# Mamba's SiLU taken from ScalarE's table in four bursts a group, 14 instead of 15 of 32 state pairs read out by GpSimd, and the conditioning products in wide form

## The chip, the cores and the metric

The kernel runs on one core of a Trainium2 chip. The core has TensorE (PE, with its weight loads PEld), VectorE (DVE), ScalarE (ACT), GpSimd (POOL) and the DMA queues, issued here by SyncE (SP) and at the start by ScalarE. All of them run at the same time, each in the order of its own program, and wait for each other by semaphores. The metric is the device time of one execution in microseconds (us); everything is float32.

## The reference, cut to what matters

`x` is 64 sequences of 128 steps and 512 channels. Layer 0 is a Mamba block with adaptive layer norm, layer 1 an attention block with FiLM; the change touches layer 0 only.

```python
ada = silu(c) @ ada_w.T + ada_b                     # c: 64 x 1024, ada: 64 x 1536
shift, scale, gate = split(ada, 3)
xn = layernorm(x) * (1 + scale) + shift
x_in, z = split(xn @ in_proj_w.T, 2)                # 1024 inner channels each
u  = silu(causal_conv4(x_in) + conv_b)
dt_r, B, C = split(u @ x_proj_w.T, [64, 80])        # 16 states
dt = softplus(dt_r @ dt_proj_w.T + dt_proj_b)
for t in range(128):                                # for each channel and state
    h = h * exp(dt_t * A) + (dt_t * u_t) * B_t
    y_t = sum_n h * C_t
y  = (y + u * D_param) * silu(z)
x1 = x + gate * (y @ out_proj_w.T)
out = attention_with_film(x1, c, mask)              # layer 1, unchanged
```

## The kernel before

**Layer 0** works on 32 groups of two sequences (`GB = 2`, 256 columns). A group has 64 slots `q`: four quarters `j` of 256 channels each, and in each quarter 16 states. Two neighbouring states are a pair, so there are 32 pairs a group and eight in a quarter. For each slot ScalarE writes a decay, exp(dt * A), in two instructions into one of four PSUM banks (`decay`, L488, tile `dA`); VectorE runs the recurrence over it in one scan of 512 columns (L732). For each pair GpSimd forms dt * u * B for both states (`scale_b`, L782, tile `dbu`, a ring of four). The finished pair is multiplied by C either on VectorE (a "D" pair: the scan stays in `dA`, product at L660 into `hC`) or on GpSimd (a "G" pair: the scan goes to `hS`, product at L793). `KINDS` says which, for each quarter. TensorE then adds `hC` or `hS` up in PSUM by transposing products (L338, tile `Y`).

A decay bank is free again when its scan is done (G) or when the product of its pair is done (D): `bank_freed` is ScalarE's wait for that. GpSimd may form `dbu` of pair p when the scans of pair p - 4 are done, and needs `du` (= dt * u, L703) of the quarter.

**Side work** of the neighbouring groups fills the same slots. `SIDE` lists it, with the slots in which TensorE issues the parts: XN (transposed norm), XI (first half of in_proj), Z (its second half), CV (the convolution), XP (x_proj), DT (dt_proj), O (out_proj). All of it goes through three PSUM banks in turn (`side`); the next user of a bank waits until ScalarE or VectorE has emptied it. Where ScalarE and VectorE take up such a piece is set by offsets from its last slot (`A_AFTER`, `D_AFTER`, `DU_AFTER`, `DT_COPY`) and by the tables `YZ_AT`, `YT_AT`, `YF_AT`, `UD_AT`, `DMM_AT` and `Q_*`. Each engine's program goes through the slots in order, so a wait in one place holds up all that stands behind it on that engine.

SiLU is x / (1 + exp(-x)). For Z and CV ScalarE computes the second factor in three steps (`staged`): exp(-x) (L532, L535), ln(1 + t) (L545), exp(-t) (L551), and VectorE multiplies (L681 into `zs`, L686 into `u`). Softplus of DT is |x|, exp, ln on ScalarE (L539, L543, L549) and max + add on VectorE (L691). All these functions lie in one table of ScalarE, so it is loaded once.

**Before the groups**, `setup` makes scale and shift for all 64 sequences on TensorE (L1369), as 64 products with 128 columns of the weight held and 64 columns streamed; VectorE turns them into `gm0` and `bm0` (L1400 to L1405). The first bodies (`at` -2 and -1) prepare group 0. **Layer 1** starts when layer 0 has ended; its chain runs on TensorE.

Of the kernel before, what the change touches and what calls it, by code (L numbers as in the profile page):

```python
# [5 lines left out]
F32 = mybir.dt.float32  # L6
# [37 lines left out]
def slot_free(i, table):  # L44
# [8 lines left out]
KINDS = ["GGDGDGDD", "GGDGDGDD", "GGDGDGDD", "GDGDDGDD"]  # L53
# [6 lines left out]
D_ACC = {4: [9, 12, 17, 18], 5: [8, 10, 12, 16, 18]}  # L60
G_ACC = {4: [8, 11, 14, 18], 3: [9, 11, 17]}
# [68 lines left out]
def mamba(nc, ctx, NG, W, C, M, io, shared, edge, x_loaded, win_z_in, win_in):  # L130
# [16 lines left out]
    tmp = [sb(f"tmp{i}", [P, D]) for i in range(2)]  # L147
# [184 lines left out]
    def _(pe):  # L332
# [41 lines left out]
        def piece(kind, j, out, part, own, par):  # L374
# [9 lines left out]
            elif kind == "Z":  # L384
                if isinstance(own, int) and own == 0 and j == 0 and part == 0:
                    pe.wait_ge(win_z_in, 16 * KD)
                b, hf = Z_BLOCK[j]
                last = pe.matmul(out[:, :], xnF[par][:, part, b * P:(b + 1) * P],  # L388
                                 W["in"][:, part, DI + hf * D:DI + (hf + 1) * D], start=(part == 0), stop=(part == KD - 1))
            elif kind == "O":  # L390
                if part % 2 == 0:
                    wait(pe, yzf_done, own * 4 + (part // 2 + 1))
                last = pe.matmul(out[:, :], yzF[part // 2][par if part < 4 else 0][:, part % 2, j, :], W["out"][:, part, :], start=(part == 0), stop=(part == KI - 1))  # L393
# [83 lines left out]
        pe.wait_ge(init_done, 6)  # L477
# [3 lines left out]
    def _(act):  # L481
        act.preload_act_table_set("natural_log_exp_and_others")
        act.wait_ge(init_done, 6)
# [8 lines left out]
        def simple(kind, j, src, own, par, part, last):  # L492
# [1004 lines left out]
```

## Time and profile before

| | us |
|---|---|
| median of three runs | 4740.08 (4734.71 to 4741.60) |
| the profiled execution's own time | 4739.39 |
| its span, first to last instruction | 4737.5 |
| first scan of layer 0 | 88.9 |
| last readout of layer 0 on GpSimd begins | 3589.8 |
| first weight product of layer 1 | 3606.5 |

The span divides into a start of about 89 us, the 32 groups of layer 0 up to about 3592 us, and layer 1. The parts of the page say, for each engine, how much of the span it was busy; a table by stage says the same for one stretch, and there an engine that is busy for the whole stretch is the candidate for the bound. A list of waits says who waited for whom. Records of one engine can overlap by a little, since the next instruction starts before the one ahead has quite ended; so the cost of one more instruction is the distance between two starts and not the mean duration of a record.

### The profile page before, as it was taken

How to read it: one execution, taken by the hardware profiler on the slowest of the kernel's cores; microseconds unless marked ns; L12 is line 12 of the kernel's file. 1: busy time of each engine (PE TensorE's matmuls, PEld its weight loads, DVE VectorE, ACT ScalarE, POOL GpSimd, SP SyncE). 2: the span in 40 equal slices, each digit the busy share in tenths (PEclk: the TensorE clock that was granted, in tenths of full speed). 3: DMA queues.
4: the chain of work that ended last, by engine and by line, in shares of the span. 5: the costliest groups of instructions: out<-in, count | busy, mean ns of one | idle time of the engine just before them, and what ended most of it. 6: DMA issues, size and time to landing. Idle time of an engine off the chain costs nothing. (4 is left out here: it accounts for less than half of the span.)

```text
span 4737.5 us, 74634 instructions
## 1 busy us (share of the span) xinstructions
PE 4324.2 (91%) x21520; PEld 3105.0 (66%) x21520; DVE 4100.3 (87%) x5030; ACT 3283.7 (69%) x7747; POOL 3852.8 (81%) x1764
## 2 busy tenths in 40 slices
PE   8898899898898988999999989888978999999998
PEld 6666666666666666666666666666665666666665
DVE  2999999999999999999999999999987666666665
ACT  3888888888888888888888888878864334343343
POOL 1999999999999999999999999999995333333332
PEclk9999999999999999999999999999999999999999
DMA  4111111111111111111111111111123223232231
GB/s 167 41 46 48 46 46 48 45 54 59 56 53 46 46 48 46 46 48 46 48 58 58 59 46 46 45 48 46 43 76 135 88 89 105 88 99 89 89 105 47
DMA packets 123161, 301.00 MB, mean 64 GB/s; under 512 B 15489, under 2 KB 20865, under 8 KB 122818
## 3 DMA queue, kind: packets, MB, share of 16 engines
q1 hardware_dynamic: 120050, 296.73, 18.5%
q8 instruction: 157, 2.57, 0.2%
q14 instruction: 186, 1.52, 0.1%
q10 hardware_dynamic: 2768, 0.17, 0.0%
HBM read 245.35 MB, written 51.51 MB: 63 GB/s over the span
## 5 line engine op out<-in xcount | busy, mean ns | idle before, releaser
L782 POOL TENSOR_TENSOR dbu<-du,bc 128x1024 f32<-128x1024 f32 x1024 | 2477.9, 2537 | 101.1 <-DMA bc<-b_scratch 86.0
L488 ACT ACTIVATE dA<-dt,c_A 128x256 f32<-128x256 f32 x4096 | 1698.5, 463 | 506.3 <-DVE hC L660 502.7
L732 DVE TENSOR_TENSOR_SCAN dA<-dA,dbu 128x512 f32<-128x512 f32 x1088 | 1288.9, 1212 | 29.9 <-ACT dA L488 28.7
L732 DVE TENSOR_TENSOR_SCAN hS<-dA,dbu 128x512 f32<-128x512 f32 x960 | 1157.6, 1212 | 94.1 <-POOL dbu L782 59.7
L793 POOL TENSOR_TENSOR hS<-hS,bc 128x1024 f32<-128x1024 f32 x480 | 1218.5, 2539 | 5.5 <-DVE hS L732 5.5
L338 PE MATMUL Y<-c_ident,hC 128*128 128x128 f32 x4352 | 581.5, 277 | 151.0 <-DVE hC L660 150.9
L338 PEld LDWEIGHTS Y<-c_ident,hC 128*128 128x128 f32 x4352 | 498.9, 142 | 287.9 <-DVE hC L660 206.7
L660 DVE TENSOR_TENSOR hC<-dA,bc 128x1024 f32<-128x1024 f32 x544 | 653.2, 1201 | 0.0
L338 PE MATMUL Y<-c_ident,hS 128*128 128x128 f32 x3840 | 509.6, 277 | 1.1 <-POOL hS L793 1.1
L412 PE MATMUL side<-xin,c_conv_w 128*128 128x256 f32 x2048 | 499.7, 378 | 0.7 <-DVE zs L681 0.7
L388 PE MATMUL side<-sh_weights,sh_tile 128*128 128x512 f32 x1024 | 497.7, 604 | 0.0
L338 PEld LDWEIGHTS Y<-c_ident,hS 128*128 128x128 f32 x3840 | 454.2, 144 | 59.6 <-issue 41.7
L405 PE MATMUL side<-sh_tile,sh_weights 128*128 128x256 f32 x2048 | 470.8, 383 | 9.0 <-ACT sh_tile L499 7.3
L393 PE MATMUL side<-c_out_w,yzF 128*128 128x512 f32 x1024 | 477.4, 593 | 0.7 <-ACT yzF L572 0.7
L952 PE MATMUL pair<-sh_weights,p_xnF 128*128 128x512 f32 x1024 | 460.0, 592 | 0.0
L412 PEld LDWEIGHTS side<-xin,c_conv_w 128*128 128x128 f32 x2048 | 372.1, 189 | 98.8 <-issue 58.2
L405 PEld LDWEIGHTS side<-sh_tile,sh_weights 128*128 128x128 f32 x2048 | 382.4, 192 | 69.3 <-ACT sh_tile L499 12.8
L1283 POOL TENSOR_TENSOR p_q<-p_q,p_qmax 128x512 f32<-128x512 f32 x64 | 67.0, 1048 | 348.8 <-DVE p_qmax L1234 348.8
L1273 POOL TENSOR_TENSOR p_xr<-p_xr,p_bo_all 128x512 f32<-128x512 f32 x64 | 79.8, 1267 | 308.3 <-DMA p_xr<-x_scratch 308.3
L952 PEld LDWEIGHTS pair<-sh_weights,p_xnF 128*128 128x128 f32 x1024 | 189.7, 190 | 201.1 <-issue 199.4
L393 PEld LDWEIGHTS side<-c_out_w,yzF 128*128 128x128 f32 x1024 | 181.2, 190 | 140.1 <-issue 135.8
L388 PEld LDWEIGHTS side<-sh_weights,sh_tile 128*128 128x128 f32 x1024 | 182.7, 194 | 115.0 <-issue 109.8
(141 smaller groups left out, 5412.8 us busy)
## 6 DMA issues: line engine op xcount, KB each, us to landing
bc<-b_scratch SPq DMA_DIRECT2D x256, 512.0 KB, 3.7
sh_tile<-in_x SPq DMA_DIRECT2D x64, 512.0 KB, 6.1
o_scratch<-oS SPq DMA_DIRECT2D x64, 256.0 KB, 2.0
sh_tile<-o_scratch SPq DMA_DIRECT2D x32, 512.0 KB, 4.7
sh_tile<-gate_scratch SPq DMA_DIRECT2D x32, 512.0 KB, 5.6
p_xr<-x_scratch SPq DMA_DIRECT2D x32, 512.0 KB, 6.8
out<-p_xr SPq DMA_DIRECT2D x32, 512.0 KB, 2.9
x_scratch<-p_x_in SPq DMA_DIRECT2D x31, 512.0 KB, 3.1
```

What stands on the lines that cost most here:

```text
L338: last = pe.matmul(Y[:, b, k * P:(k + 1) * P], src[:, n, k, b * P:(b + 1) * P], C["ident"][:, :], start=False, stop=False, is_transpose=Tr ...
L388: last = pe.matmul(out[:, :], xnF[par][:, part, b * P:(b + 1) * P], W["in"][:, part, DI + hf * D:DI + (hf + 1) * D], start=(part == 0), st ...
L393: last = pe.matmul(out[:, :], yzF[part // 2][par if part < 4 else 0][:, part % 2, j, :], W["out"][:, part, :], start=(part == 0), stop=(pa ...
L405: last = pe.matmul(out[:, half * GT:(half + 1) * GT], W["in"][:, k, e * P:(e + 1) * P], xnF[par][:, k, :], start=(k == 0), stop=(k == KD - 1))
L412: last = pe.matmul(out[:, half * GT:(half + 1) * GT].rearrange("p (b t) -> p b t", b=GB), W["conv"][:, e, t, :], xin[j % 2][:, half, :, t: ...
L488: last = act.activation(dA[:, q % A_RING, e, :], dt[j % 2][:, e, :], ACT.Exp, scale=C["A"][:, 2 * j + e, n:n + 1])
L660: dve.tensor_tensor(hC[C_SLOT[i]][:, :, :, :], dA[:, k:k + 2, :, :], bc[:, 1, n:n + 2, :].unsqueeze(2).broadcast_to([P, 2, 2, GT]), ALU.mu ...
L732: dve.tensor_tensor_scan(out.rearrange("p e t -> p (e t)"), dA[:, q % A_RING, :, :].rearrange("p e t -> p (e t)"), dbu[(q // 2) % B_RING][ ...
L782: gps.tensor_tensor(dbu[p % B_RING][:, :, :, :], du[j % 2][:, :, :].unsqueeze(1).broadcast_to([P, 2, 2, GT]), bc[:, 0, n:n + 2, :].unsquee ...
L793: gps.tensor_tensor(h, h, bc[:, 1, n:n + 2, :].unsqueeze(2).broadcast_to([P, 2, 2, GT]), ALU.mult).then_inc(hcP_done, 1)
L952: last = pe.matmul(out[:, :], lhs(k), w[:, k, :], start=(k == 0), stop=(k == KD - 1))
L1273: gps.tensor_tensor(xr[:, b, :], xr[:, b, :], bo[:, :], ALU.add).then_inc(s["xb_done"], 1)
```

## The change

- `KINDS` has 14 G pairs and 18 D pairs a group (15 and 17 before), in another pattern; the fourth `hS` buffer goes with it.
- SiLU of Z and CV is one function of ScalarE, straight from PSUM into `zs` and `u`. It lies in another table than exp and ln, so `BURSTS` puts one Z and one CV together at four slots of a group, with a table load ahead of them and one behind. VectorE has no part in it any more. Z is cut by quarters instead of by sequence and half.
- An `hC` product follows the second scan of its pair directly (`R_AFTER = 1`; it stood one scan later). The DT step and `du` stand in the same slot.
- All tables of slots are new. `tmp` is one tile, `yzF` is single except for quarter 0.
- In `setup` the conditioning products hold the 64 sequences and stream 512 columns of the weight (16 products); VectorE copies the result to SBUF and TensorE turns it back (eight transposes). The clearing of rows of the dt weight moves from the start of `mamba` to `setup`.

```diff
-KINDS = ["GGDGDGDD", "GGDGDGDD", "GGDGDGDD", "GDGDDGDD"]
+KINDS = ["GGDGGDDD", "GDGDGDDD", "GDGDGGDD", "GDGDDDGD"]
-D_ACC = {4: [9, 12, 17, 18], 5: [8, 10, 12, 16, 18]}
+D_ACC = {4: [9, 14, 19, 19], 5: [10, 10, 13, 13, 18]}
...
+    ("Z", 1, 0, [0, 0, 1, 2]),
+    ("CV", 1, 1, [0, 0, 1, 2]),
...
+    ("O", 0, -1, [9, 9, 9, 9, 10, 10, 10, 10]),
...
+    ("DT", 0, 1, [49]),
+    ("CV", 0, 2, [53, 53, 54, 54]),
+    ("Z", 0, 1, [53, 54, 55, 55]),
...
+BURSTS = [
+    (6, [("Z", 1, 0), ("CV", 1, 1)]),
+    (22, [("Z", 2, 0), ("CV", 2, 1)]),
+    (36, [("CV", 3, 1), ("Z", 3, 0)]),
+    (58, [("Z", 0, 1), ("CV", 0, 2)]),
+]
...
+STEP1, STEP2, DT_AFTER, DU_AFTER, COPY_AFTER = 1, 2, 4, 4, 7
+R_AFTER = 1
+YZ_AT = [20, 33, 52, 68]
-S_RING = 3
+S_RING = 4
...
+        def take_functions(name):
+            if functions[0] != name:
+                act.preload_act_table_set(name)
+                functions[0] = name
...
+        def soft(kind, j, src, own, par):
+            if kind == "Z":
+                take_functions(SILU)
                 wait(act, filled[kind], nth(kind, j, own))
+                wait(act, yz_done, own * 4 + j - 1)
+                act.activation(zs[j % 2][:, :, :].rearrange("p b c -> p (b c)"), src[:, :], ACT.Silu).then_inc(zs_done, 1)
+            elif kind == "CV":
+                take_functions(SILU)
+                wait(act, filled[kind], nth(kind, j, own))
...
+                for e in range(2):
+                    last = act.activation(u[par][:, 2 * j + e, :], src[:, e * GT:(e + 1) * GT], ACT.Silu,
+                                          bias=C["cb"][:, 2 * j + e:2 * j + e + 1])
...
-                        t = 16 * j + 2 * p + 2
+                        t = 16 * j + 2 * p + R_AFTER
                         if q == t % UNITS and inside(at, -(t // UNITS)):
                             readout(g - t // UNITS, j, m)
...
-                    last = pe.matmul(ps[:, i, k, :], ada[:, c, s:s + P], cT[:, c, :],
-                                     start=(c == 0 and i == 0 and k == 0), stop=(c == KC - 1), skip_group_check=True)
+                last = pe.matmul(ps[i][0:NB, :], cT[:, c, :], ada[:, c, i * D:(i + 1) * D], start=(c == 0), stop=(c == KC - 1))
...
+        dve.memset(W["dt"][RANK:XD, :], 0.0)
+        for i in range(2):
+            dve.wait_ge(mod_done, i + 1)
+            dve.tensor_copy(mod[0:NB, i, :], ps[i][0:NB, :]).then_inc(mod_copied, 1)
+        dve.wait_ge(mod_turned, 2)
```

What the order on ScalarE was at slots 16 to 26 of group 0 (dA is the decays, four instructions for two slots; L535, L545 and L551 are the three steps of a CV piece, L539, L543 and L549 those of a DT piece, L572 copies `Y` out):

```order
L488 ACTIVATE dA<-dt1,c_A 128x256 x4
L565 ACTIVATE uD<-u0,c_dcol 128x256 x2
L488 ACTIVATE dA<-dt1,c_A 128x256 x4
L535 ACTIVATE tmp1<-side0,c_ncb 128x256 x2
L488 ACTIVATE dA<-dt1,c_A 128x256 x4
L545 ACTIVATE tmp1<-tmp1 128x512
L551 ACTIVATE tmp1<-tmp1 128x512
L488 ACTIVATE dA<-dt1,c_A 128x256 x4
L572 ACTIVATE yzF00<-Y 128x512
```

And now, at slots 16 to 25 (L547 and L554 are the SiLU of Z and CV, L591 the copy of `Y`, L628 and L630 belong to the norm):

```order
L504 ACTIVATE dA<-dt1,c_A 128x256 x16
L495 ACT_TABLE_LOAD
L547 ACTIVATE zs0<-side2 128x512
L554 ACTIVATE u1<-side1,c_cb 128x256 x2
L591 ACTIVATE yzF0a<-Y 128x512
L495 ACT_TABLE_LOAD
L628 ACTIVATE lnv<-mv,c_eps 128x2
L630 ACTIVATE rstd<-lnv 128x2
L504 ACTIVATE dA<-dt1,c_A 128x256 x4
```

The steps of CV stood one by one between the decays; now a block with two table loads stands between the decays of slot 23 and those of slot 24.

VectorE at slots 22 to 26 of group 0, before (the rows named after three tensors, into `dA` or `hS`, are scans; `hC1` and `hC2` are products of D pairs):

```order
L732 SCALAR_TENSOR_TENSOR hS0<-dA,dbu3 128x512
L660 TENSOR_TENSOR hC1<-dA,bc 128x1024
L732 SCALAR_TENSOR_TENSOR hS0<-dA,dbu3 128x512
L732 SCALAR_TENSOR_TENSOR dA<-dA,dbu0 128x512 x2
L732 SCALAR_TENSOR_TENSOR hS1<-dA,dbu1 128x512
L660 TENSOR_TENSOR hC2<-dA,bc 128x1024
```

And now, at slots 22 to 25:

```order
L729 SCALAR_TENSOR_TENSOR dA<-dA,dbu3 128x512
L748 BN_AGGR mv<-stats 128x2 x2
L729 SCALAR_TENSOR_TENSOR dA<-dA,dbu3 128x512
L678 TENSOR_TENSOR hC2<-dA,bc 128x1024
L729 SCALAR_TENSOR_TENSOR hS2<-dA,dbu0 128x512 x2
```

Before, the product of a D pair stood behind the first scan of the pair after it (`hC1` behind a scan into `hS0`); now it stands right behind the second scan of its own pair.

ScalarE at the start of group 0, before (L557 is the copy of dt, L499 the norm of the next group):

```order
L549 ACTIVATE tmp0<-tmp0 128x512
L557 ACTIVATE dt0<-side2 128x4x127
L488 ACTIVATE dA<-dt0,c_A 128x256 x4
L499 ACTIVATE sh_tile2<-side0,c_bm0,c_gm0 128x128 x2
L499 ACTIVATE sh_tile2<-side1,c_bm0,c_gm0 128x128 x2
```

And now:

```order
L570 ACTIVATE tmp<-tmp 128x512
L576 ACTIVATE dt0<-side2 128x4x127
L495 ACT_TABLE_LOAD
L547 ACTIVATE zs0<-side0 128x512
L515 ACTIVATE sh_tile2<-side1,c_bm0,c_gm0 128x128 x2
L515 ACTIVATE sh_tile2<-side2,c_bm0,c_gm0 128x128 x2
L495 ACT_TABLE_LOAD
L504 ACTIVATE dA<-dt0,c_A 128x256 x4
```

Two table loads, a SiLU of Z and half of the norm now stand ahead of the first decays of the layer.

## Rows read from the trace of the kernel before

**Rows 1.** Table by stage: each engine's busy time in each stretch, then clock, DMA.

```profile
core 0: us, PE busy (x) PEld busy (x) DVE busy (x) ACT busy (x) POOL busy (x), PEclk, DMA share, GB/s
...
1000.00:1500.00 500.00, 454.42 (x2394) 338.04 (x2393) 486.02 (x503) 412.03 (x955) 500.00 (x217) 0.99 0.14 46
```

**Rows 2.** Timeline of POOL: start, duration, line, operation, tiles, count.

```profile
1000.14 6.97 POOL L782 TENSOR_TENSOR dbu<-du,bc 128x1024 f32<-128x1024 f32 x3
1007.08 2.35 POOL L793 TENSOR_TENSOR hS<-hS,bc 128x1024 f32<-128x1024 f32 x1
```

**Rows 3.** Table by stage, one period of a group.

```profile
1002.39:1111.22 108.83, 98.68 (x522) 73.70 (x521) 105.91 (x110) 89.03 (x207) 108.83 (x48) 0.98 0.15 50
```

**Rows 4.** Who waited for whom, VectorE, 300 to 3300 us: total us, times, longest.

```profile
DVE hS L732 <- POOL dbu L782: 55.8, 54, 1.5
DVE hS L732 <- ACT dA L488: 14.6, 15, 1.2
DVE dA L732 <- ACT dA L488: 9.6, 27, 0.4
```

**Rows 5.** Groups by line, that same period: count | busy us, mean ns | idle before.

```profile
L488 ACT ACTIVATE dA<-dt,c_A 128x256 f32<-128x256 f32 x128 | 53.1, 463 | 15.0 <-DVE hC L660 15.0
L551 ACT ACTIVATE tmp<-tmp 128x512 f32<-128x512 f32 x8 | 5.0, 625 | 0.1
L545 ACT ACTIVATE tmp<-tmp 128x512 f32<-128x512 f32 x8 | 5.0, 620 | 0.0
```

**Rows 6.** Timeline of ACT in layer 1, around a table load.

```profile
3700.49 0.63 ACT L1078 ACTIVATE p_hF<-p_hp 128x512 f32<-128x512 f32 x1 [0.57 <-DVE p_hp L1154]
3701.14 1.28 ACT L1079 ACT_TABLE_LOAD   x1
3702.43 1.08 ACT L1083 ACTIVATE p_qF<-pair 128x512 f32<-128x512 f32 x2
```

**Rows 7.** Timeline of DVE in that period.

```profile
1048.86 0.85 DVE L686 SCALAR_TENSOR_TENSOR u<-side,c_cb,tmp 128x256 f32<-128x256 f32 x2
1049.63 2.33 DVE L732 TENSOR_TENSOR_SCAN dA<-dA,dbu 128x512 f32<-128x512 f32 x2
1051.88 0.67 DVE L681 TENSOR_TENSOR zs<-side,tmp 128x512 f32<-128x512 f32 x1
1052.47 1.21 DVE L732 TENSOR_TENSOR_SCAN dA<-dA,dbu 128x512 f32<-128x512 f32 x1
1053.59 1.20 DVE L660 TENSOR_TENSOR hC<-dA,bc 128x1024 f32<-128x1024 f32 x1
```

**Rows 8.** Timeline of DVE: the last pair of layer 0.

```profile
3592.17 1.22 DVE L732 TENSOR_TENSOR_SCAN dA<-dA,dbu 128x512 f32<-128x512 f32 x1
3593.42 1.22 DVE L660 TENSOR_TENSOR hC<-dA,bc 128x1024 f32<-128x1024 f32 x1
```

**Rows 9.** Timeline of the start, all engines.

```profile
6.62 27.54 PE L1369 MATMUL mod<-c_cT,ada 128*128 128x64 f32 x128 [6.62 <-DMA ada<-in_adaT]
...
34.28 1.10 DVE L1400 TENSOR_SCALAR t<-mod,c_one_plus,c_cols 128x64 f32<-128x64 f32 x4 [6.93 <-PE mod L1369]
...
38.75 0.91 DVE L649 MEMSET c_dt_w<- 32x1024 f32 x1 [0.27 <-issue]
...
39.72 1.97 PE L399 MATMUL side<-c_ident,sh_tile 128*128 128x128 f32 x8 [5.55 <-DVE c_dt_w L649]
```

**Rows 10.** Timeline, waits of DVE and POOL in group 0 and in the last group.

```profile
108.31 2.35 DVE L732 TENSOR_TENSOR_SCAN dA<-dA,dbu 128x512 f32<-128x512 f32 x2 [11.13 <-ACT dA L488]
...
110.74 2.35 POOL L782 TENSOR_TENSOR dbu<-du,bc 128x1024 f32<-128x1024 f32 x1 [5.81 <-DVE dA L732]
...
3536.53 2.35 POOL L782 TENSOR_TENSOR dbu<-du,bc 128x1024 f32<-128x1024 f32 x1 [8.44 <-DVE du L703]
```

**Rows 11.** Chain that ended last, in order of time: start, us, what.

```profile
3674.05 13.73 PE pair L952 x32
```

More of the change, by code:

```diff
@@ L120 @@
 C_RING = 3
-S_RING = 3
+S_RING = 4
 C_SLOT = [i % C_RING for i in range(ND)]
-S_SLOT = [(G_BASE[j] + i + sum(j >= at for at in (1, 3)[:-NGP % S_RING])) % S_RING for j in range(4) for i in range(len(G_PAIRS[j]))]
+S_SLOT = [(G_BASE[j] + i + j * (-NGP % S_RING) // 3) % S_RING for j in range(4) for i in range(len(G_PAIRS[j]))]
 PAIRS = UNITS // 2
+LOG_EXP, SILU = "natural_log_exp_and_others", "silu_and_others"
 FAR = 1e30
@@ L146, in mamba @@
     u = [sb(f"u{i}", [P, KI, GT]) for i in range(2)]
-    tmp = [sb(f"tmp{i}", [P, D]) for i in range(2)]
     xd = sb("xd", [XD + 1, GT])
@@ L386, in piece @@
                     pe.wait_ge(win_z_in, 16 * KD)
-                b, hf = Z_BLOCK[j]
-                last = pe.matmul(out[:, :], xnF[par][:, part, b * P:(b + 1) * P],
-                                 W["in"][:, part, DI + hf * D:DI + (hf + 1) * D], start=(part == 0), stop=(part == KD - 1))
+                for k in two:
+                    last = pe.matmul(out[:, half * 2 * P:(half + 1) * 2 * P], xnF[par][:, k, half * P:(half + 1) * P],
+                                     W["in"][:, k, DI + j * 2 * P:DI + (j + 1) * 2 * P], start=(k == 0), stop=(k == KD - 1))
             elif kind == "O":
@@ new lines, in softplus @@
+        def softplus(step, j, src, own):
+            take_functions(LOG_EXP)
+            if step == 0:
+                wait(act, filled["DT"], nth("DT", j, own))
+                wait(act, dt_done, own * 4 + j)
+                act.activation(tmp[:, :], src[:, :], ACT.Abs).then_inc(abs_done, 1)
+            elif step == 1:
+                wait(act, abs_done, own * 4 + (j + 1))
+                act.activation(tmp[:, :], tmp[:, :], ACT.Exp, scale=-1.0).then_inc(exp_done, 1)
+            else:
+                wait(act, exp_done, own * 4 + (j + 1))
+                act.activation(tmp[:, :], tmp[:, :], ACT.Ln, bias=1.0).then_inc(log_done, 1)
@@ L639, in body @@
                 beside(q + 1)
+            if inside(at, 0):
+                take_functions(LOG_EXP)
         over_groups(act, body)
@@ L697, in make_gate, with step @@
             dve.tensor_tensor(oS[1][0:NB, :], dA[0:NB, 3, :, :].rearrange("p e t -> p (e t)"), oS[0][0:NB, :], ALU.add).then_inc(gate_v, 1)
+        def step(j, src, own):
+            wait(dve, log_done, own * 4 + (j + 1))
+            dve.scalar_tensor_tensor(src[:, :], src[:, :], 0.0, tmp[:, :], ALU.max, ALU.add).then_inc(dt_done, 1)
         def step_times_u(j, src, own, par):
@@ L752, in body @@
                     last.then_inc(stats_done, 1)
-                for (kind, j, d, end, bk, s, off), of, go in side:
-                    if kind == "DT" and q == end + DU_AFTER - off:
+                for (kind, j, d, end, bk, off), of, go in side:
+                    if q == end + DT_AFTER - off:
+                        step(j, bank[bk], go + d)
+                    if q == end + DU_AFTER - off:
                         step_times_u(j, bank[bk], go + d, (of + d) % 2)
-                    if kind in D_AFTER and q == end + D_AFTER[kind] - off:
-                        side_dve(kind, j, bank[bk], tmp[(sig_base[of] + s) % 2], go + d, (of + d) % 2)
         over_groups(dve, body)
```

203 lines of the change are left out of this document (76 added, 127 removed).

## The prediction

> **What bounds the kernel now.** I read the table by stage first. In the middle of layer 0 POOL is busy for 500.00 of 500 us, DVE for 486.02, PE for 454.42, ACT for 412.03 [rows 1]. The timeline of POOL shows no gap between its instructions: three take 6.94 us from start to start, 2.31 us each, whether it is a `dbu` or a readout [rows 2]. A group has 32 + 15 = 47 of them, and the period of a group is 108.83 us [rows 3], which is 47 x 2.315. So POOL sets layer 0. The second engine is close: DVE is busy for 105.91 us of that period [rows 3], and its waits over 300 to 3300 us are 55.8 us for POOL and 24.2 us for ACT's decays, in 27.6 periods 2.0 and 0.9 us each [rows 4]. ACT is busy for 89.03 us and waits 15.0 us for DVE to give back a decay bank [rows 3, 5]: it runs as far ahead as the four banks let it. Layer 1's chain is PE alone, 0.43 us a record of 512 columns, and is not touched [rows 11].
>
> **POOL.** One readout less a group: 46 x 2.315 = 106.5 us instead of 108.8. Over 32 groups that is **74.1 us**, as long as POOL never waits. Nothing in the change touches what one POOL instruction costs.
>
> **DVE.** Removed: four Z products at 0.59 us and four CV pairs at 0.77 us from start to start [rows 7], 5.4 us. Added: one more `hC` product, 1.12 us [rows 7]. There is an addition that the diff shows only as `R_AFTER = 1`: each `hC` now follows directly on the scan whose result it reads, and has to wait for its end. Where nothing depends, an instruction starts 1.12 us after the one ahead; the only place in before where a product follows its own scan is the last pair, and there it is 1.25 us [rows 7, 8]. Lower bound: 0, if the ring of scans hides it; upper 0.13. I take the one row: 18 x 0.13 = 2.3 us. The four `du` directly behind their DT step get the same, 0.5 us. Sum: 105.9 - 5.4 + 1.1 + 2.3 + 0.5 = **104.4 us** of 106.5. DVE is as nearly full as before, with 2.1 us a group to spare (2.9 before).
>
> **ACT.** Removed: L545 and L551 for Z and CV, 5.0 + 5.0 us a group [rows 5]. The first step becomes the SiLU, at the same size: in layer 1 a SiLU of 512 columns takes 0.63 us [rows 6]. Added: eight table loads a group. A load takes 1.28 us, begins 0.02 us after the SiLU ahead has ended, and the next instruction starts 0.01 us after it [rows 6]; eight are 10.4 us. Sum: 89.0 - 10.0 + 0.3 + 10.4 = 89.7 us, as much as before. What is new is that it comes in blocks of 1.28 + 0.6 + 0.8 + 1.28 = 4.0 us, in which no decay is made. The Trainium skill (ScalarE: Activation LUTs, What ACT_TABLE_LOAD costs) gives 1283 ns for the load, as here, and another 1380 ns of drain for every switch. By that, eight switches would be 21.3 us, ACT would have 100.7 us a group and a block would last 6.8 us; the row shows no such drain.
>
> **Does a block starve DVE?** I walk through the one at slot 22, which also has the copy of `Y` and the two norm steps. Let time 0 be the end of the `hC` product that frees the banks for slots 22 and 23. ACT: decays to 1.8 (53.1 / 128 = 0.415 us each [rows 5]), load to 3.0, Z to 3.6, CV to 4.4, copy to 5.0, load to 6.3, two small norm steps to 6.9, first decay of slot 24 ready at 7.7. DVE in that time: scan 20, the gate product, two norm statistics of 0.6, scans 21, 22, 23 and the next `hC`, 4 x 1.13 + 0.6 + 1.2 + 0.2 + 1.25 = 7.8. So it arrives just as the decay does; slot 26, whose banks come free only at 7.8 and behind which two more side steps stand, may cost 0.4. For slot 6 (block behind a G pair, which gives its banks back early) I get 6.3 for ACT and 6.4 for DVE, for slot 36 5.7 and 6.4, for slot 58 7.2 and 7.0. About 0.6 us of waits in sum, beside the 0.9 us that DVE waits for decays today [rows 4]. 104.4 + 1.0 to 1.5 = 105.4 to 105.9, under 106.5: POOL keeps the bound, with its `dbu` ring of four pairs between it and DVE's small delays. I allow 0.1 us a group for places where it doesn't, 3 us in all.
>
> **PE** has the same streaming as before (Z as 16 products of 256 instead of 4 of 512 columns in each quarter, at the same us per column), 98.7 us busy of then 106.5 [rows 3]. It has to finish Z and CV before their block; what a late one costs is a rival below.
>
> **Start.** The 64-column products of `setup` take 27.54 us, 0.43 us for each of 64 pairs of records [rows 9]. The wide ones are 16 pairs at 2 x 0.43 [rows 11], 13.8 us, and end near 20.4. DVE is ready at 34.28 - 6.93 = 27.35 [rows 9]; then come the clearing that moved here (0.91 [rows 9]), two copies near 0.7 each and four plus four transposes, about 1 us: 30.7 instead of 34.28, 3.6 us earlier. The 0.91 us clearing stood just ahead of the first transpose at 39.72 [rows 9] and is gone from there. Together -4.5. Up to the first `dbu` a CV loses two ScalarE steps and DVE's product (0.62 + 0.63 + 0.85, [rows 5, 7]), which counts for the last one; against that XI, its copy and CV of one quarter now follow each other on PE, four copies near 0.6 exposed. I take 0.
>
> **Group 0 pays.** Before, DVE waited 11.13 us and POOL 5.81 us here, as ACT stood at XI copies ahead of slot 4 [rows 10]. Now two loads, Z (which PE makes only behind the gate product) and half of the norm stand ahead of the first decay, and a head block and the block of slot 6 follow at once. Decays of slots 0 and 1 come about 11 us later after the end of the DT product than they did, the XI copies about 5 us later; three blocks then add some 8 us on ACT, of which its spare time gives back part. I take POOL's start as +9 us, with 3 to 15 as bounds. **Last group:** POOL waited 8.44 us for `du` [rows 10], as O and the FiLM product shared PE's slots 14 to 21 ahead of the DT product. O is now at 9 and 10; I take half of the wait, -4, bounds -8 to +4.
>
> **Sum.** Against the profiled execution: 4739.4 - 74.1 + 3 - 4.5 + 9 - 4 = 4668.8; the median of the runs is 0.7 above it, so **4670 us**.
>
> **The rivals.** (1) *DVE takes the bound.* It has 2.1 us a group to spare. If the waits for decays are 3.5 us a group (0.9 us a block), the period is 107.9 and the gain 30 us: 4712. For it: at slots 22 and 58 the two sides of the walk meet within 0.2 us, and 2.3 us of DVE's sum rest on one row. Against: the slots of the blocks stand where DVE has other work. Chance 0.18 for anything from 4690 to 4730. (2) *The blocks cost more than the gain*: slower than before. It decides from 108.8 - 104.4 = 4.4 us of waits a group, 1.1 us a block. It happens if PE delivers Z or CV late, since then ACT stands inside the block with SiLU's table loaded and no decay can be made: PE is 93% busy, and the block of slot 36 takes a Z whose last part PE issues at slot 36, just behind O 1 and CV 3. At 2 us late in each block: 104.4 + 1 + 8 = 113.4, +147 us, 4885 us. Chance 0.07. (3) *A table switch costs a drain in the middle of a busy ACT queue*, which the rows of layer 1, where ACT has idle time ahead, might not show: blocks of 6.8 us, 2.8 us late each, 104.4 + 1 + 11 = 116.4, +243 us, near 4980. This is the case that the page named above would give. Chance 0.03. (4) *The gain is given back in no measurable way* (group 0 worse than 15 us and DVE's waits near break-even together), 4731 to 4749: 0.04.
>
> **How the numbers follow.** POOL-bound: 0.68, from 4655 (group 0 +3, last group -8, no slack used) to 4685. With rival 1 the range to hold eight in ten is 4655 to 4722. A measurement of this kernel tells about 0.2% (9.5 us) from no change. Faster by more: 0.68 + 0.18 = 0.86; within: 0.04; slower: 0.10.
>
> **What the profile after would show.** Right: POOL busy all of a middle stretch with 46 instructions in 106.5 us; DVE near 104.4 busy; its waits for decays under 2 us a group; table loads of 1.28 us with no gap around them; first `dbu` near 82, and waits of POOL in group 0 of 20 us instead of 11. Wrong: any wait of POOL for DVE in the middle of layer 0 (rival 1); waits of ACT for PE inside a block (rival 2); a gap next to a load (rival 3); `hC` starting 1.12 us after its own scan would show DVE's sum 2.3 us too high.

## The result, and the profile after

The changed kernel takes **4697.39 us** (median of four runs, 4694.11 to 4699.91) beside 4737.96 us of the kernel before (median of four runs too, 4734.71 to 4741.60): ratio 0.9916, 95% interval 0.9904 to 0.9927. It is 0.84% or 40.6 us faster; 4670 was predicted, in a range of 4655 to 4722. The profiled execution took 4697.85 us, with a span of 4696.0.

A group in the middle, the row that answers to [rows 3] (us of PE, PEld, DVE, ACT, POOL, then clock and DMA):

```profile
2078.04:2184.60 106.56, 98.39 (x552) 80.42 (x552) 103.10 (x99) 90.89 (x199) 106.56 (x47) 0.98 0.15 51
```

The period is 106.56 us as forecast, and POOL has no gap in it. The page's rows of the `hC` products and of the table loads:

```profile
L678 DVE TENSOR_TENSOR hC<-dA,bc 128x1024 f32<-128x1024 f32 x576 | 705.2, 1224 | 64.9 <-DVE dA L729 15.5
...
L495 ACT ACT_TABLE_LOAD x263 | 337.4, 1283 | 12.3 <-PEq L1443 7.7
```

But not all groups are like that one. POOL's list of waits from 300 to 3300 us, which has no entry in the kernel before:

```profile
POOL dbu L779 <- DVE du L704: 25.0, 12, 2.9
POOL hS L790 <- DVE hS L729: 1.5, 4, 0.5
```

26.5 us, where the prediction allowed 3. In POOL's timeline they stand in pairs; one of the six pairs, behind an ordinary group:

```profile
2280.78 9.29 POOL L779 TENSOR_TENSOR dbu<-du,bc 128x1024 f32<-128x1024 f32 x4
...
2389.36 9.33 POOL L779 TENSOR_TENSOR dbu<-du,bc 128x1024 f32<-128x1024 f32 x4 [1.64 <-DVE du L704]
...
2417.35 9.31 POOL L779 TENSOR_TENSOR dbu<-du,bc 128x1024 f32<-128x1024 f32 x4 [2.44 <-DVE du L704]
```

The first of a pair is the first `dbu` of quarter 1, the second that of quarter 2, and pairs begin at 665, 1096, 1528, 1959, 2389 and 2819 us: every 431 us, which is four groups, and six times. The middle of the program is a loop over four groups with seven turns (`with eng.Fori(0, (NG - 4) // 4)`, bodies `at` 1 to 4), so it jumps back six times. What the engines do at that place, from 2357 us on (timelines of ACT, PE and DVE, one after the other):

```profile
2357.24 3.27 ACT L504 ACTIVATE dA<-dt,c_A 128x256 f32<-128x256 f32 x8
2363.40 1.67 ACT L504 ACTIVATE dA<-dt,c_A 128x256 f32<-128x256 f32 x4 [2.89 <-DVE dA L729]
...
2372.20 1.28 ACT L495 ACT_TABLE_LOAD   x1
2374.17 0.60 ACT L547 ACTIVATE zs<-side 128x512 f32<-128x512 f32 x1 [0.68 <-DVE yz L687]
...
2377.94 0.60 ACT L591 ACTIVATE yzF<-Y 128x512 f32<-128x512 f32 x1 [2.13 <-PE Y L378]
...
2364.43 3.43 PE L395 MATMUL side<-sh_weights,sh_tile 128*128 128x256 f32 x8 [5.08 <-issue]
...
2366.71 4.57 DVE L729 TENSOR_TENSOR_SCAN hS<-dA,dbu 128x512 f32<-128x512 f32 x4 [2.48 <-ACT dA L504]
```

"issue" is idle time in which nothing that the profile shows was waited for. TensorE stands 5.08 us, and its next eight products take 3.43 us instead of 1.89, as the granted clock is 0.58 behind the stop, between its levels of 1.2 and 2.4 GHz (0.5 and 1.0); from 2368 us on it is 1.00. The table by stage has it in the third column from the end:

```profile
2364.00:2368.00 4.00, 3.57 (x10) 2.96 (x11) 1.52 (x3) 3.49 (x10) 4.00 (x3) 0.58 0.51 180
```

ScalarE issues no decay for 2.9 us. The profile puts this down to a scan (`<-DVE dA L729`), which had ended at 2362.88; in a group without a jump there is no stop at this place, and twelve decay instructions follow each other (experiment 1). DVE gets its decays 2.48 us late, then waits 0.99 us for TensorE ahead of the gate product and 2.01 us behind the block of slot 6. That block lasts from 2372.20 to 2379.85, 7.65 us instead of 4.4, as the `Y` copy in it waits 2.13 us for TensorE. So DVE comes 5.0 us late to `du`, here that of quarter 2, in the group ahead and in this one (period 106.56 us):

```profile
2305.01 0.69 DVE L704 TENSOR_TENSOR du<-side,u 128x512 f32<-128x512 f32 x1
...
2416.58 0.69 DVE L704 TENSOR_TENSOR du<-side,u 128x512 f32<-128x512 f32 x1
```

The parts, against the kernel before:

| | forecast | measured | from |
|---|---|---|---|
| one readout less, 32 groups | -74.1 | -73.8 | POOL's 32 groups without their waits, 3411.2 instead of 3485.0 us |
| start, up to the first `dbu` | -4.5 | -3.5 | 82.99 instead of 86.47 us |
| POOL's waits in group 0 | +9 | +7.2 | 19.4 instead of 12.2 us |
| POOL's waits in the middle | +3 | +26.5 | the list above |
| POOL's waits in the last groups | -4 | +1.0 | 9.5 instead of 8.4 us |
| behind POOL's last instruction of layer 0 | 0 | +1.1 | 1146.5 instead of 1145.4 us |
| sum | -70.6 | -41.5 | 41.5 between the profiled executions |

### The profile page after: what moved, and what is told of

It reads as the page before. It is cut to its first block and busy times, and to the rows that moved or that the text cites. A ratio compares the mean times of both kernels' runs of the same rounds, so it can differ in the third digit from the quotient of the medians.

```text
span 4696.0 us, 75508 instructions
## 1 busy us (share of the span) xinstructions
PE 4326.6 (92%) x22456; PEld 3319.5 (71%) x22456; DVE 4017.1 (86%) x4680; ACT 3351.9 (71%) x7497; POOL 3779.0 (80%) x1732
## 5 line engine op out<-in xcount | busy, mean ns | idle before, releaser
L779 POOL TENSOR_TENSOR dbu<-du,bc 128x1024 f32<-128x1024 f32 x1024 | 2391.2, 2359 | 118.1 <-DMA bc<-b_scratch 82.5
L729 DVE TENSOR_TENSOR_SCAN dA<-dA,dbu 128x512 f32<-128x512 f32 x1152 | 1355.1, 1212 | 26.2 <-POOL dbu L779 21.1
L729 DVE TENSOR_TENSOR_SCAN hS<-dA,dbu 128x512 f32<-128x512 f32 x896 | 1040.6, 1205 | 63.5 <-ACT dA L504 49.2
L790 POOL TENSOR_TENSOR hS<-hS,bc 128x1024 f32<-128x1024 f32 x448 | 1057.0, 2359 | 19.9 <-DVE hS L729 19.9
L678 DVE TENSOR_TENSOR hC<-dA,bc 128x1024 f32<-128x1024 f32 x576 | 705.2, 1224 | 64.9 <-DVE dA L729 15.5
L345 PEld LDWEIGHTS Y<-c_ident,hC 128*128 128x128 f32 x4608 | 534.7, 145 | 111.9 <-DVE hC L678 94.7
L345 PEld LDWEIGHTS Y<-c_ident,hS 128*128 128x128 f32 x3584 | 416.7, 144 | 181.8 <-POOL hS L790 157.5
L395 PE MATMUL side<-sh_weights,sh_tile 128*128 128x256 f32 x2048 | 504.7, 388 | 27.8 <-issue 27.8
L395 PEld LDWEIGHTS side<-sh_weights,sh_tile 128*128 128x128 f32 x2048 | 386.1, 195 | 79.2 <-issue 30.0
L412 PEld LDWEIGHTS side<-sh_tile,sh_weights 128*128 128x128 f32 x2048 | 385.1, 195 | 61.8 <-issue 10.3
L400 PE MATMUL side<-c_out_w,yzF 128*128 128x512 f32 x896 | 399.3, 596 | 0.7 <-ACT yzF L591 0.7
L495 ACT ACT_TABLE_LOAD x263 | 337.4, 1283 | 12.3 <-PEq L1443 7.7
```

Source lines behind the costliest of these rows:

```text
L345: last = pe.matmul(Y[:, b, k * P:(k + 1) * P], src[:, n, k, b * P:(b + 1) * P], C["ident"][:, :], start=False, stop=False, is_transpose=Tr ...
L395: last = pe.matmul(out[:, half * 2 * P:(half + 1) * 2 * P], xnF[par][:, k, half * P:(half + 1) * P], W["in"][:, k, DI + j * 2 * P:DI + (j ...
L400: last = pe.matmul(out[:, :], yzF[part // 2][par if part < 2 else 0][:, part % 2, j, :], W["out"][:, part, :], start=(part == 0), stop=(pa ...
L412: last = pe.matmul(out[:, half * GT:(half + 1) * GT], W["in"][:, k, e * P:(e + 1) * P], xnF[par][:, k, :], start=(k == 0), stop=(k == KD - 1))
L495: act.preload_act_table_set(name)
L678: dve.tensor_tensor(hC[C_SLOT[i]][:, :, :, :], dA[:, k:k + 2, :, :], bc[:, 1, n:n + 2, :].unsqueeze(2).broadcast_to([P, 2, 2, GT]), ALU.mu ...
```

## The experiments

Medians are of the runs of a kernel; ratios are to runs of the kernel before on the same chip, with 95% intervals. "Without the loop" means that the 28 middle groups are written out.

**1. No loop, and twice the jumps.** The edit, for all engines at once:

```
-        with eng.Fori(0, (NG - 4) // 4) as i:
-            for at in range(1, 5):
-                body(i * 4 + at, at)
+        for at in range(1, NG - 3):
+            body(at, at)
```

> The changed kernel with the 28 middle groups written out instead of a loop of seven turns of four groups; every engine's instructions and tables are the same. Theory A (the loop's jump): in the trace of the changed kernel POOL waits for du twice after each of the six jumps back, 4.4 us a jump, because ACT issues nothing for about 2.9 us at the jump and the slack between du and its first use in the quarters 1 and 2 is smaller than that. Without jumps these waits go: 4697 - 26 = 4671 us, POOL without a wait from 130 to 3400 us. Rival B (the waits come from something else that recurs every four groups, such as data or side work): 4697, the same waits at the same places. Rival C (the code written out has to be fetched all the time and costs more than the jumps): over 4697.

4670.12 us, ratio 0.9862 (0.9845 to 0.9878). POOL's list of waits from 300 to 3300 us is empty. At the same place of the program as above:

```profile
2338.39 4.87 ACT L503 ACTIVATE dA<-dt,c_A 128x256 f32<-128x256 f32 x12
2343.19 0.90 ACT L583 ACTIVATE uD<-u,c_dcol 128x256 f32<-128x256 f32 x2
...
2340.55 1.89 PE L394 MATMUL side<-sh_weights,sh_tile 128*128 128x256 f32 x8
```

ScalarE goes through from one group to the next with twelve decay instructions in a row where it had stopped after eight, and TensorE's products of `Z` 1 have no wait ahead of them. Theory A holds to 1 us, and B and C fall.

With a loop over two groups (`(NG - 4) // 2`, `range(1, 3)`), 13 jumps:

> The changed kernel with a loop of 14 turns of two groups instead of seven of four: 13 jumps back instead of 6. Theory A: seven more jumps at 4.4 us, 4697 + 31 = 4728 us, a pair of POOL waits for du every 217 us. Theory A with saved-up slack (DVE may need more than two groups to catch up): more than that, up to 4740. Rival B: 4697.

4726.98 us, ratio 0.9979 (0.9970 to 0.9989): 29.6 us for seven more jumps, 4.2 each, beside 27.3 us for the first six, 4.5 each. POOL's waits from 300 to 3300 us:

```profile
POOL dbu L779 <- DVE du L704: 42.4, 21, 2.8
POOL hS L790 <- DVE hS L729: 12.8, 13, 1.5
```

TensorE's idle time put down to issue is 27.8 us in 6 places in the changed kernel and 56.3 us in 13 here: 4.6 and 4.3 us a jump.

**2. The same in the kernel before.** The loop over two groups there:

> The kernel before with a loop of 14 turns of two groups instead of seven of four. Its POOL waits 0.9 us in sum in the middle of layer 0, though it makes the same jumps. Theory A: its slack (du of quarter 1 in slot 7 instead of 12) covers the jump, so seven more of them cost 0 to 2 us: 4738 to 4740. If the jump had a price by itself on POOL, 7 x 2 to 4 us: 4752 to 4768.

4733.65 us, ratio 0.9995 (0.9985 to 1.0004): nothing. This is ScalarE in the kernel before, at the jump:

```profile
2386.43 0.84 ACT L535 ACTIVATE tmp<-side,c_ncb 128x256 f32<-128x256 f32 x2 [0.18 <-PE side L412]
2389.79 1.67 ACT L488 ACTIVATE dA<-dt,c_A 128x256 f32<-128x256 f32 x4 [2.52 <-issue]
```

So a stop of 2.5 us was in the trace from which the prediction was made, and cost nothing there. The same place one group earlier, and TensorE at the jump, show why:

```profile
2279.68 1.67 ACT L488 ACTIVATE dA<-dt,c_A 128x256 f32<-128x256 f32 x4 [1.32 <-DVE hC L660]
...
2388.60 1.34 PE L338 MATMUL Y<-c_ident,hC 128*128 128x128 f32 x8 [2.21 <-DVE hC L660]
```

ScalarE stands there for a decay bank for 1.32 us in every group without a jump, and 1.9 to 2.5 us at the six jumps: a jump adds 0.6 to 1.2 us, DVE then waits as long for decays, and POOL not at all. TensorE stands 2.2 us for `hC` there in every group, with a jump or without; the stop of 4.2 to 5.1 us that it makes in the changed kernel is not in this trace. The new order has no idle time at that place on either engine, so the stops come through. Why TensorE's own stop is so much longer there is not shown.

**3. `du` earlier by moving the DT products.**

```
     ("Z", 1, 0, [0, 0, 1, 2]),
     ("CV", 1, 1, [0, 0, 1, 2]),
-    ("XI", 2, 1, [3, 5, 6, 8]),
-    ("DT", 1, 0, [8]),
+    ("DT", 1, 0, [3]),
+    ("XI", 2, 1, [7, 8, 8, 8]),
...
+    ("DT", 2, 0, [17]),
     ("Z", 2, 0, [18, 19, 19, 20]),
-    ("XI", 3, 1, [21, 21, 22, 22]),
-    ("DT", 2, 0, [24]),
+    ("XI", 3, 1, [23, 23, 24, 24]),
```

> The changed kernel with the DT product of quarter 1 at slot 3 instead of 8 and of quarter 2 at slot 17 instead of 24 (du then in slots 7 and 21 instead of 12 and 28), XI 2 and XI 3 behind them; the loop as it is. Theory A: POOL's waits for du in the middle (26.5 us), most of the 6.0 us of them in group 0 and of the 4.6 us in the last group go: 4697 - 26 - 4 - 3 = 4664 us. Rival D (DVE itself is the bound around a jump, and the waits for du only show it; DVE has 2 us a group to spare and the loss would come out elsewhere, as waits for scans): 4685 to 4697.

4844.60 us, ratio 1.0225 (1.0208 to 1.0242): far off both. The waits for `du` are gone from POOL's list, but TensorE's list from 300 to 3300 us now begins:

```profile
PE side L412 <- ACT zs L547: 130.5, 27, 4.9
```

The three side banks go round in the order of the list. By the swap `XI` 2 gets the bank of `Z` 1, which ScalarE empties only inside the block of slot 6. TensorE comes there before the block and stands 4.8 us in each group, with everything behind it. The edit did not only move `du`, so its time decides nothing about theory A; it shows what a late TensorE or a late block costs: 4.6 us a group. One thing can be read from it: with `du` of quarter 1 in slot 7, as in the kernel before, a group with a jump is still 5 us longer than its neighbours (116.5 us beside 111.5).

**4. Is the gain the readout alone?** The version without the loop, with quarter 1 of `KINDS` as before (15 G pairs):

```
-KINDS = ["GGDGGDDD", "GDGDGDDD", "GDGDGGDD", "GDGDDDGD"]
+KINDS = ["GGDGGDDD", "GGDGDGDD", "GDGDGGDD", "GDGDDDGD"]
```

> The changed kernel without the loop (4670 us), with 15 of 32 pairs on GpSimd as before the change (one D pair of quarter 1 becomes a G pair); SiLU, bursts, slots and setup stay new. Theory A (the gain of the middle is the one readout less, and nothing else): POOL is full again with 47 instructions of 2.315 us, 32 x 2.315 = 74 us more, 4744 us. Rival E (the new SiLU or the slots gain something by themselves): under 4735.

4740.21 us, ratio 1.0006 (0.9997 to 1.0016): 70.1 us more than with 14, of 74.1. New SiLU, blocks and slots bring nothing as long as POOL bounds; DVE's waits for decays, 2.3 us a group there from 1000 to 3000 us, cost nothing either. (Outside the middle, POOL's waits in the groups 0 and 31 also differ: 27.0 us here and 28 to 29 with 14.)

**5. Was the SiLU needed for it?** The kernel before with 14 G pairs, first with its loop, then without:

```
-KINDS = ["GGDGDGDD", "GGDGDGDD", "GGDGDGDD", "GDGDDGDD"]
+KINDS = ["GGDGDGDD", "GDGDGDDD", "GGDGDGDD", "GDGDDGDD"]
```

> The kernel before with 14 instead of 15 of 32 pairs on GpSimd, and nothing else changed: SiLU in three steps with VectorE's products. Theory A: POOL would need 106.5 us a group, but DVE needs 105.9 + 1.1 = 107.0 us and has 0.9 us of waits for decays: period 107.9 instead of 108.8, 4738 - 29 = 4709 us, DVE full and POOL waiting. If the slack of POOL's ring is not enough for two engines that are both full, 4715 to 4730. Rival F (POOL sets the time even so, and the SiLU part of the change was not needed): 4738 - 74 = 4664 us.

4767.86 us, ratio 1.0064 (1.0047 to 1.0081): slower than before, beyond what theory A allowed.

> The kernel before with 14 G pairs (4768 us with the loop) and the middle groups written out. In the trace of the version with the loop the period is 109.1 us in most groups and 1.5 to 2 us longer around a jump. Theory A (DVE is full there, so each of six jumps costs 2 to 4 us): 4743 to 4756 us, still not faster than before, with a period of 109.1 us: 107.0 of work and 2.2 us of waits for decays. If the 30 us by which it was slower than before came from the jumps alone: 4738 or less.

4728.26 us, ratio 0.9982 (0.9972 to 0.9991). One group of it:

```profile
2107.91:2216.85 108.94, 98.56 (x521) 73.64 (x521) 106.40 (x111) 88.81 (x207) 106.78 (x47) 0.98 0.15 49
```

DVE is full: 106.4 us busy, and 1.8 us of waits for decays a group (34.0 us in the 18.4 periods from 1000 to 3000 us), twice those of [rows 4]; that this is so because a D pair gives its banks back later than a G pair was not tested by itself. The row is of the longer kind of group: periods of 109.0 and 107.9 us (2.3 and 1.3 us of waits for decays) alternate, 108.5 in the mean instead of 108.9. The jumps cost 39.6 us here, 6.6 each, more than the forecast 2 to 4; they are spread over all four groups of a turn. So with this pattern and the old slots the readout gains 8 us (4728.3 beside 4736.5 on the same chip) without the loop and loses with it. DVE's part of the SiLU has to go before POOL's 106.5 us can be reached; what the whole change adds without the loop is 4728.3 - 4670.1 = 58 us. Other slots for the old SiLU were not tried.

**6. Is there room in the blocks?** Without the loop, and between the two SiLUs of a block:

```
+                            if i == 1:
+                                take_functions(LOG_EXP)
+                                act.activation(spare[:, :], C["eps"][:, :], ACT.Exp)
                             soft(kind, j, bank[bk], g + d, (at + d) % 2)
```

> The changed kernel without the loop (4670 us), in which each burst of two SiLUs is cut in two: behind the first SiLU the table of exp and ln is loaded, one exp of a single column runs into a spare tile, and SiLU's table is loaded again. That adds 2 x 1.28 us and about 0.2 us to each of the four blocks, as much as a drain at each of the eight switches would have. Theory A (the walk of the prediction: the sides meet within 0.2 to 1 us in the blocks): DVE waits about 2 us more in each block, 104.4 + 1 + 8 = 113 us a group, near 4880 us, 4840 to 4910. Rival G (the four banks and ACT's spare 17 us a group absorb it): DVE's 2.3 us a group of slack are not used up, 4670 to 4690.

4938.16 us, ratio 1.0424 (1.0407 to 1.0442), worse than theory A's range. A group takes 115.22 us:

```profile
2102.34:2217.56 115.22, 102.68 (x552) 85.22 (x552) 103.31 (x100) 101.92 (x211) 106.85 (x47) 0.94 0.14 47
```

and DVE's waits for decays from 1000 to 3000 us are

```profile
DVE hS L732 <- ACT dA L504: 148.0, 52, 3.0
DVE dA L732 <- ACT dA L504: 30.0, 33, 2.5
```

178 us in 17.4 periods, 10.3 us a group or 2.6 a block for 2.9 us of added length (7.35 instead of 4.43 us, each with one copy in it). The blocks have next to no room, as the walk said. ScalarE as a whole is not full (101.9 of 115.2 us), and that does not help.

**7. One more readout to VectorE.** Without the loop, 13 G pairs:

```
-KINDS = ["GGDGGDDD", "GDGDGDDD", "GDGDGGDD", "GDGDDDGD"]
+KINDS = ["GGDGDDDD", "GDGDGDDD", "GDGDGGDD", "GDGDDDGD"]
```

> The changed kernel without the loop (4670 us), with 13 instead of 14 pairs on GpSimd (one G pair of quarter 0 becomes a D pair). POOL needs 45 x 2.315 = 104.2 us a group. In the middle of the kernel without the loop DVE waits 2.3 us a group for POOL and 0.2 us for decays, so its own work is about 104.0 to 104.2 us; one more product makes 105.4. Theory A: DVE is the bound, 105.4 + 0.2 to 1 us of waits = 105.6 to 106.4 us a group, 4642 to 4667 us, and POOL waits 1 to 2 us a group. Rival (with both engines full the ring of four no longer covers, and decays come late since the bank of a D pair is free later): slower than 4670, up to 4700.

4662.90 us, ratio 0.9844 (0.9828 to 0.9861), a period of 105.93 us. The same with each `hC` product one scan later:

```
-R_AFTER = 1
+R_AFTER = 2
```

> The version without the loop and with 13 G pairs (4663 us, period 105.9 us, DVE full), with each hC product one scan later, as before the change (R_AFTER = 2). Theory H (the direct successor costs DVE 0.13 us for each of 19 products, and nothing else changes): DVE needs 2.4 us a group less, POOL's 104.2 us bound it, 4663 - 31 x 1.7 = 4610 us, at most 4625. Theory A (the four blocks on ACT have no room: a D pair that gives its two banks back 1.1 us later makes each block end 1.1 us later for DVE): 2.4 us gained and 4 x 1.1 us or more of new waits for decays, 4663 + 31 x 2 = 4725 us, from 4690 to 4760.

4847.61 us, ratio 1.0235 (1.0218 to 1.0252): the sign of theory A, with three times its price. DVE waits 151 us for decays from 1000 to 3000 us (1.2 before the edit). The two banks of a D pair come back later, and the blocks turn this into waits. Theory H's saving is there all the same: without its waits DVE needs 102.7 us a group instead of 105.2. Without `hC` directly behind its scan this version with the blocks is slower than the kernel before; the prediction had this placing only as a cost.

In the version with 13 G pairs POOL waits 1.6 us a group for a `du`. I took it for that of quarter 1 and moved its DT product:

```
-    ("XI", 2, 1, [3, 5, 6, 8]),
-    ("DT", 1, 0, [8]),
+    ("XI", 2, 1, [3, 5, 6, 7]),
+    ("DT", 1, 0, [7]),
```

> The version without the loop and with 13 G pairs (4663 us), with the DT product of quarter 1 at slot 7 instead of 8 (XI 2 ends at 7 too), so du of quarter 1 stands in slot 11 instead of 12. There POOL waits 1.6 us for du in each group, and DVE 0.7 us for POOL 19 slots earlier. Theory A: both go, the period is DVE's work alone, 105.9 - 0.7 = 105.2 us, 4663 - 22 = 4641 us. Rival I (DT 1 takes the side bank that the block of slot 6 frees; TensorE stands there until the block's end, so du comes no earlier, and the products behind come later): 4660 to 4690, with a wait of TensorE of 1 to 2 us a group at the DT product.

4665.38 us, ratio 0.9852 (0.9836 to 0.9869): no gain. The wait was for `du` of quarter 2, in slot 28 behind the block of slot 22, and the moved steps of ScalarE cost DVE 1.1 us of waits for decays. (`DT` 2 ends at slot 24, and DVE takes it up four slots later.) For quarter 2 VectorE alone is moved:

```
-                    if q == end + DT_AFTER - off:
+                    if q == end + DT_AFTER - (j == 2) - off:
                         step(j, bank[bk], go + d)
-                    if q == end + DU_AFTER - off:
+                    if q == end + DU_AFTER - (j == 2) - off:
```

> The version without the loop and with 13 G pairs (4663 us), in which VectorE takes the DT step and du of quarter 2 one slot earlier (27 instead of 28); ScalarE and TensorE as they are. In its trace POOL's wait of 1.6 us in each group is for this du, and ScalarE's last step for it ends 2.2 us before VectorE takes it up. Theory A: POOL's wait becomes 0.5 us, DVE's 0.7 us for POOL goes, period 105.9 - 0.7 = 105.2 us, 4663 - 22 = 4641 us. Rival J (the time comes back as DVE waits for decays behind the blocks, as when the DT product of quarter 1 was moved): 4655 to 4665 us.

**4625.77 us**, ratio 0.9768 (0.9752 to 0.9784), the fastest of all. A group before and after this edit, in the two versions:

```profile
2050.71:2156.64 105.93, 96.98 (x552) 79.02 (x552) 104.24 (x100) 90.52 (x199) 104.33 (x46) 1.00 0.15 51
```

```profile
2035.21:2140.32 105.11, 98.28 (x552) 80.57 (x552) 104.16 (x101) 90.55 (x199) 104.33 (x46) 0.98 0.15 51
```

DVE waits neither for POOL nor, but for 0.3 us in 2000, for ScalarE: its own work is the period. POOL's wait is 0.8 us a group. 0.82 us a group is 25 of the 37 us. Another 8.6 us are in the last group, where POOL's waits fall from 20.9 to 12.3 us; this was not expected.

## Why the prediction was right, and where it was off

**What bounds, and the readout: right.** POOL sets the period, 46 x 2.315 us, in every group without a jump, and experiment 4 gives 70 us for the one readout. As a whole the change is 0.84% faster where 1.4% were forecast: the mechanism held, and a term that the sum had nearly at nothing took 26.5 us back.

**VectorE's sum: right.** In the middle groups it waits 2.3 us a group for POOL and 0.2 for ACT in the version without the loop, so its own time is 106.6 - 2.5 = 104.1 us; 104.4 was forecast. It is busy for 103.1 us. The rest, 1.0 us, are short gaps ahead of the `hC` products. Where a scan, its neighbour and `hC` follow each other, `hC` starts 1.25 us after the second scan, as in [rows 8]:

```profile
2329.86 2.33 DVE L729 TENSOR_TENSOR_SCAN dA<-dA,dbu 128x512 f32<-128x512 f32 x2
2332.23 1.23 DVE L678 TENSOR_TENSOR hC<-dA,bc 128x1024 f32<-128x1024 f32 x1
2333.37 2.33 DVE L729 TENSOR_TENSOR_SCAN dA<-dA,dbu 128x512 f32<-128x512 f32 x2
```

2332.23 - 2329.86 is 2.37 for a scan at 1.12 and this step. That the step costs this much is shown by experiment 7, where DVE's own time falls by 2.5 us for 19 products when they stand one scan later. What the term left out is the other side of `R_AFTER = 1`: experiment 7 prices it at 185 us in the version with 13 G pairs.

**ScalarE and the blocks: right.** 90.9 us a group instead of 89.7, and a block without a wait, here with an `XI` copy in it:

```profile
2333.96 1.28 ACT L494 ACT_TABLE_LOAD   x1
2335.26 0.60 ACT L546 ACTIVATE zs<-side 128x512 f32<-128x512 f32 x1
2335.75 0.83 ACT L553 ACTIVATE u<-side,c_cb 128x256 f32<-128x256 f32 x2
2336.46 0.61 ACT L520 ACTIVATE xin<-side 128x512 f32<-128x512 f32 x1
2337.09 1.28 ACT L494 ACT_TABLE_LOAD   x1
```

A load starts 0.02 us after what is ahead of it and is followed at once, in a busy queue as in layer 1 [rows 6]. By these rows a switch costs 1.28 us. The Trainium skill (ScalarE: Activation LUTs, What ACT_TABLE_LOAD costs) adds 1380 ns of drain to each; no run here shows it. The rival built on it (4980 us) is answered by experiment 6, in which that much time was really added: 4938 us.

**The start: right within 1 us.** The wide products and what follows them:

```profile
6.58 16.70 PE L1365 MATMUL mod<-ada,c_cT 128*64 128x512 f32 x32 [6.58 <-DMA ada<-in_adaT]
...
28.21 0.91 DVE L1399 MEMSET c_dt_w<- 32x1024 f32 x1 [0.25 <-issue]
29.14 1.28 DVE L1402 COPY mod<-mod 64x512 f32<-64x512 f32 x2
...
31.20 1.10 DVE L1405 TENSOR_SCALAR t<-turned,c_one_plus,c_cols 128x64 f32<-128x64 f32 x4 [0.78 <-PE turned L1371]
...
35.46 1.97 PE L406 MATMUL side<-c_ident,sh_tile 128*128 128x128 f32 x8 [4.30 <-DVE xd L667]
```

The products end at 23.3 instead of 20.4 us (0.52 us a record where [rows 11] have 0.43), which is hidden. The chain goes on at 31.20 instead of 30.7, the first transpose starts 4.3 us earlier than in [rows 9], and 0.8 us of it are lost again before the first `dbu`.

**Group 0: right.** The timeline, with ScalarE's part first:

```profile
82.46 1.28 ACT L495 ACT_TABLE_LOAD   x1
89.07 0.60 ACT L547 ACTIVATE zs<-side 128x512 f32<-128x512 f32 x1 [5.33 <-PE side L395]
...
93.27 1.23 DVE L729 TENSOR_TENSOR_SCAN hS<-dA,dbu 128x512 f32<-128x512 f32 x1 [11.45 <-ACT dA L504]
...
107.21 2.34 DVE L729 TENSOR_TENSOR_SCAN hS<-dA,dbu 128x512 f32<-128x512 f32 x2 [11.02 <-ACT dA L504]
...
109.62 2.35 POOL L790 TENSOR_TENSOR hS<-hS,bc 128x1024 f32<-128x1024 f32 x1 [8.71 <-DVE hS L729]
```

SiLU's table is loaded and `Z` is not there: rival 2's mechanism, at the place where the prediction had put its price. POOL waits 19.4 us, 20 were forecast.

**The last group: wrong sign.** -4 was taken because `O` no longer shares TensorE's slots with the FiLM product. It is now `Z` 2, in slots 18 to 20, that shares them:

```profile
3478.08 0.60 ACT L547 ACTIVATE zs<-side 128x512 f32<-128x512 f32 x1 [5.27 <-PE side L395]
...
3484.08 2.34 DVE L729 TENSOR_TENSOR_SCAN hS<-dA,dbu 128x512 f32<-128x512 f32 x2 [6.86 <-ACT dA L504]
...
3486.50 2.37 POOL L790 TENSOR_TENSOR hS<-hS,bc 128x1024 f32<-128x1024 f32 x1 [2.10 <-DVE hS L729]
...
3492.51 9.28 POOL L779 TENSOR_TENSOR dbu<-du,bc 128x1024 f32<-128x1024 f32 x4 [3.64 <-DVE du L704]
```

The block waits 5.27 us with the wrong table loaded, and the waits for `du` come back behind it. The step did not ask which other pieces stand in the FiLM product's slots.

**The middle: the term that was mis-sized**, 3 us instead of 26.5. The sum was made from one period of 106.5 us and multiplied, and nothing in it was about the loop, though the stop of 2.5 us stands in the trace of before. That the loop is the cause is shown by experiment 1. The reason given for the 3 us was that the `dbu` ring of four pairs lies between POOL and DVE's small delays. It does for scans, but POOL cannot form a `dbu` without `du`, and `du` of quarter 2 is done only 0.5 us ahead of its first use in an ordinary group (2305.70 and 2306.25 us). It stood nearly as close in the kernel before (slot 28 in both, 0.7 to 1.0 us ahead). What is new is that DVE comes late: 5.0 us at the `du` of quarters 1 and 2 behind the jump at 2359 us (4.2 to 6.1 at the six jumps), from the three waits named in the section on the result, where in the kernel before no `du` of quarter 2 was late by as much as 0.2 us. POOL lost 4.4 us there: 0.35 us for a scan, 1.64 at quarter 1, whose `du` has 3.1 us to spare (2277.71 and 2280.78 us), and 2.44 more at quarter 2. The slot of `du` in quarter 1 did go from 7 to 12, but this only sets at which of the two quarters POOL stands first: a `du` of quarter 2 that is 5.0 us late with 0.5 to spare gives the 4.4 us by itself. This last step is worked out from the trace; no experiment moved the jump or `du` alone.

**Where luck helped.** For its own mechanism the prediction gave 4655 to 4685, and 4697 lies above that. It is inside 4655 to 4722 only by the width that was added for rival 1. And the 4670.12 us without the loop meets the forecast in part by chance: there the last group is worse than forecast by 4.4 us, and the middle (0 instead of 3) and group 0 (7.6 instead of 9) are better by as much.

**Rival 1** (DVE takes the bound, 4690 to 4730) covers the measured time by its number, and its sign came true: POOL waits for DVE in the middle of layer 0. Its mechanism, waits for decays at the blocks of every group, did not: in the version without the loop DVE has 2.3 us to spare in every middle group. Rival 2's sign, a wait for TensorE inside a block, stands in group 0, in the last group and behind each jump.

## What to carry to other kernels

A sum over one period is only as good as the places that are not in the period: list the loop's jumps, the first and the last groups, and ask in each which buffer covers the stop. When a table of slots is written anew, compare for every product the time at which it is made with the time at which the bounding engine takes it up, and look for the smallest difference: a product that is ready 0.5 us early costs nothing until something else is late, and then all but those 0.5 us. A stop that falls into idle time is hidden; look what a new order leaves idle at that place. An engine with 15% of idle time can still have no room at all in one place, and taking two instructions of one quarter up a single slot earlier was worth 37 us here, more than the jumps.

## What the runs showed of the hardware

- At a loop's jump in the changed kernel TensorE stands 4.2 to 5.1 us without a wait that the profile shows (3.8 to 5.5 with thirteen jumps), and ScalarE stops for 1.6 to 3.1 us where it goes through in other groups. The Trainium skill (Advanced Engine Details and Errata, Control Flow Timing) gives about 108 ns for a compare-and-branch; in this kernel, with bodies of four groups, TensorE's stop is over thirty times that. The profile's table of DMA has packets of two queues that it calls "instruction": from 2359 to 2369 us, around a jump,

```profile
q14 instruction: 5, 0.04, 2.3%
q8 instruction: 2, 0.03, 1.8%
```

(packets, MB, share), and none in the same stretch of the group ahead, 2252.5 to 2262.5 us. In the whole run there are 348 such packets with six jumps and 395 with thirteen. That the engines wait for them is likely and not shown.
- The price of a jump depends on who is covered: 4.5 us in the changed kernel, 6.6 in the kernel before with 14 G pairs, where VectorE is full, and nothing that can be measured in the kernel before, where seven more jumps changed the time by less than its scatter.
- Written out, with 28 groups of code, nothing was lost: 4670 us, with no time put down to issue on TensorE or ScalarE between 200 and 3400 us.
